# Second feed-forward of a two-layer gated cross-attention block: tokens sorted by expert, one expert per tile, in place of all experts masked

## The reference, cut to what matters

```python
def _L1_ffn_ref(x, gate_w, gate_b, W1, b1, W2, b2):
    logits = jnp.einsum('bld,de->ble', x, gate_w) + gate_b
    probs = jax.nn.softmax(logits, axis=1)
    idx = jnp.argmax(probs, axis=-1)
    out = jnp.zeros_like(x)
    for e in range(N_EXP):
        h = jax.nn.gelu(jnp.einsum('bld,df->blf', x, W1[e]) + b1[e], approximate=False)
        y = jnp.einsum('blf,fd->bld', h, W2[e]) + b2[e]
        out = out + jnp.where((idx == e)[..., None], y, jnp.float32(0.0))
    return out
...
x = x + jnp.tanh(g_xattn[1]) * _L1_xattn_ref(ctx_1024, _layernorm(x, axis=-1), ...)
x = x + jnp.tanh(g_ffn[1]) * _L1_ffn_ref(_layernorm(x, axis=-1), ...)
```

## Time and profile before

| | |
|---|---|
| median of 3 runs | 760.32 us (759.6 to 761.9) |
| profiled execution, device time | 757.69 us |
| its span | 755.6 us (2.1 us of the time lie around it) |
| busy share of the span | PE 93%, PEld 70%, DVE 73%, ACT 47%, POOL 45% |
| mean granted clock of TensorE | 0.986 of full speed |

### The profile page before, as it was taken

How to read it: one execution, slowest core, us unless ns; L and a number is a source line. 1 busy time by engine, 2 the same in 40 slices (tenths; PEclk the granted TensorE clock), 3 DMA queues, 4 the chain that set the end, 5 groups by cost and what they waited for, 6 DMA issues and landing times.

```text
span 755.6 us, 14538 instructions
## 1 busy us (share of the span) xinstructions
PE 699.8 (93%) x5642; PEld 530.3 (70%) x5642; DVE 552.8 (73%) x1089; ACT 356.9 (47%) x531; POOL 337.9 (45%) x421
## 2 busy tenths in 40 slices
PE   5789999999988898999999999999999988999896
PEld 5666666666877776767777677776777655887895
DVE  5767887774798877977668766688866886687544
ACT  3657667665344335555444445445534545120300
POOL 3374434410442215666656666567665774100000
PEclk9689999999999999999999999999999999999999
DMA  8100000000600030000000000000000000000000
GB/s 182 20 1 2 3 1 2 2 2 2 223 1 0 1 95 18 1 2 1 2 1 2 1 2 1 1 2 1 3 1 2 1 2 0 1 8 1 8 8 7
DMA packets 25586, 11.58 MB, mean 15 GB/s; under 512 B 11856, under 2 KB 24224, under 8 KB 25392
## 3 DMA queue, kind: packets, MB, share of 16 engines
q1 hardware_dynamic: 24512, 10.60, 5.5%
q10 hardware_dynamic: 1008, 0.07, 0.1%
HBM read 10.08 MB, written 0.52 MB: 14 GB/s over the span
## 4 chain that ended last, share of the span: by engine, by line
PE 72%; DVE 21%; issue 4%; ACT 1%; DMA 1%; SPq 0%; DVEq 0%; ACTq 0%
PE ps L1754 69%; DVE o L1458 3%; DVE pmax L1445 2%; DVE mx L1128 2%; PE ps L1765 1%; DVE kql L1433 1%; DVE exm L1324 1%; DVE ysum L1591 1%; DVE pmax L1442 1%; DMA raw<-in_L_xattn_Wproj_dram 1%; DVE rs_t L1005 1%; PE ps L1858 1%; DVE w_l L1666 0%; DVE sel L1584 0%; DVE wsel L1321 0%
## 5 line engine op out<-in xcount | busy, mean ns | idle before, releaser
L868 ACT ACTIVATE p<-ps 128x1024 f32<-128x1024 f32 x96 | 96.2, 1026 | 148.1 <-PE ps L1754 148.1
L1754 PE MATMUL ps<-p,v 128*64 128x256 f32 (+1 forms) x1280 | 125.0, 387 | 0.6 <-DVE xr L1154 0.6
L600 POOL TENSOR_TENSOR acc<-p 128x256 f32<-128x256 f32 x128 | 91.7, 748 | 74.8 <-ACT p L868 74.5
L1754 PE MATMUL ps<-kqh 64*128 64x256 f32 (+1 forms) x640 | 109.9, 369 | 13.2 <-DVE pmax L1442 3.5
L606 POOL TENSOR_TENSOR acc<-acc,p 128x256 f32<-128x256 f32 x128 | 92.0, 751 | 59.3 <-ACT p L868 59.2
L1442 DVE TENSOR_REDUCE pmax<-ps 128x2 f32<-128x1024 f32 x64 | 78.2, 1222 | 36.3 <-PE ps L1754 36.0
L1128 DVE TENSOR_REDUCE mx<-ps 128x1 bf16<-128x512 f32 x128 | 82.5, 687 | 25.1 <-PE ps L1754 24.4
L1754 PEld LDWEIGHTS ps<-p,v 128*64 128x64 f32 (+1 forms) x1280 | 66.8, 127 | 47.2 <-issue 16.5
L1754 PEld LDWEIGHTS ps<-kqh 64*128 64x128 f32 x640 | 61.7, 190 | 42.4 <-issue 34.6
L555 POOL TENSOR_SCALAR q<-qst,rmask 128x256 fp32r<-128x256 f32 x64 | 58.9, 940 | 58.3 <-ACT qst L628 58.3
L732 ACT ACTIVATE p<-ps 128x1024 f32<-128x1024 f32 x64 | 65.5, 1026 | 23.1 <-PE ps L1754 21.3
(11 more groups left out here) (294 smaller groups left out, 1587.5 us busy)
## 6 DMA issues: line engine op xcount, KB each, us to landing
w<-in_L_ffn_W_dram SPq DMA_DIRECT2D x1, 2048.0 KB, 12.0
wt<-in_L_ffn_W_dram SPq DMA_DIRECT2D x4, 512.0 KB, 6.1
ctx_all<-in_ctx_dram SPq DMA_DIRECT2D x4, 256.0 KB, 5.6
raw_kv<-in_L_xattn_Wkv_dram SPq DMA_DIRECT2D x1, 1024.0 KB, 4.8
raw<-in_L_ffn_B_dram SPq DMA_DIRECT2D x9, 64.0 KB
xr<-in_x_dram SPq DMA_DIRECT2D x4, 128.0 KB, 3.9
raw_q<-in_L_xattn_Wq_dram SPq DMA_DIRECT2D x1, 512.0 KB, 5.7
wout<-in_L_xattn_Wout_dram SPq DMA_DIRECT2D x1, 512.0 KB, 7.0
```

Source lines behind the costliest of these rows:

```text
L600: ins = pool.tensor_tensor(acc1[:, at], p1[:, s, 0, at], p1[:, s, 1, at], ALU.add)
L868: act.activation(p1[:, g % 2, u, :], bank(2 * (n % 2), 2), ACT.Exp, scale=SCALE1).then_inc(a_exp1.sem, 1)
L1754: return pe.matmul(o, lhsT, rhs, start=start, stop=stop)
```

## The change

Tokens are handled in two sets: batches 0 to 2 (768 tokens, 6 tiles) and batch 3 (256 tokens, 2 tiles). For each set, DVE and PE find the expert of every token, its rank among the tokens of that expert (a triangular matmul, `rank1`), and a slot: each expert's slots begin at a multiple of 128, so that a tile of 128 slots belongs to one expert. 768 tokens need at most 13 such tiles and 256 tokens at most 9, and all 22 are always computed. POOL scatters the normed tokens (`xnA`, `xnB3`) by slot number to scratch memory, one indirect transfer per 128 tokens (`scattered`); SP reads the slots back in groups of up to four tiles (`slots_in`); PE turns them (`slots_turn`), ACT and DVE split them (`slots_high`, `slots_low`). PE reads the number of each tile's expert into registers (`experts_in`) and takes that expert's weights through an address in a register. For a tile `up1` has 4 matmuls of 512 columns, `hidden_turn` 4 transposes, `down1` 4 of 256 columns and 5 of 128. The result `y1` of each tile is written to scratch memory (`slots_out`), and when a set is done POOL gathers the rows of its tokens (`gathered`, 6 and 2 indirect transfers), DVE adds them to `xr` and SP writes them out.

Besides: the low and high parts of W1 are now made in attention steps 8 to 10 and 14 to 18, one expert in each, and those of W2 in steps 29 to 31; batch 2's `outputs1` goes one step ahead; routing of the first set goes into steps 24 to 31. The scatter of the first set stands on POOL ahead of the sums of step 31.

```diff
+    SETS = (range(B - 1), range(B - 1, B))
+    TOKEN_TILES = tuple(TQ * len(z) for z in SETS)
+    SLOT_TILES = tuple((n * P + E * (P - 1)) // P for n in TOKEN_TILES)
...
+        W1_PAIRS = (8, 9, 10, 14, 15, 16, 17, 18)
+        W2_PAIRS = (G1 - 3, G1 - 2)
+        TURN_SLOTS = (1, 5, 9, 11, 14, 18)
...
+            def scattered(z, of):
+                pool.wait_ge(s_zero.sem, 32)
+                pool.wait_ge(d_route.sem, d_route.after(z, 4))
+                for t in range(TOKEN_TILES[z]):
+                    pool.indirect_dma_start(
+                        out=xs_dram[z], out_offset=bass.IndirectOffsetOnAxis(ap=slot_u[z][:, t:t + 1], axis=0),
+                        in_=of[:, t, :], in_offset=None).then_inc(s_scatter[z].sem, 16)
...
             for g in range(G1):
                 s = g % 2
+                if g == G1 - 1:
+                    scattered(0, xnA)
...
+            spread_hot(0)
+            scattered(1, xnB3)
+            spread_hot(1)
+            gathered(0)
+            gathered(1)
...
+            slots_high(0)
+            gelu(0)
+            for tile in range(SLOTS_ALL):
+                if tile + 1 < SLOTS_ALL:
+                    gelu(tile + 1)
+                hidden_high(tile)
+                if tile >= 1:
+                    output_part(tile - 1)
...
+                if tile == 5:
+                    softmax(1)
+            output_part(SLOTS_ALL - 1)
...
+                mm(o, xs_h[:, tile, :], of_expert(w1_h), True, False)
+                mm(o, xs_h[:, tile, :], of_expert(w1_l), False, False)
+                mm(o, xs_l[:, tile, :], of_expert(w1_h), False, False)
+                mm(o, hot[:, tile, :], biases_hl[:, 0:F], False, True).then_inc(e_up.sem, 1)
...
+            expert = list(experts_in(0))
+            slots_turn(0)
+            up1(0)
+            outputs1(B - 1)
+            for tile in range(SLOTS_ALL):
+                if tile + 1 < SLOTS_ALL:
+                    up1(tile + 1)
+                hidden_turn(tile)
+                if tile >= 1:
+                    down1(tile - 1)
+                if tile in TURN_SLOTS:
+                    slots_turn(TURN_SLOTS.index(tile) + 1)
...
+                if tile == SLOT_TILES[0] - 2:
+                    expert += list(experts_in(1))
+            down1(SLOTS_ALL - 1)
```

More of the change, by code:

```diff
@@ L219, in flamingo @@
[L219 to L226, removed]
@@ L494, in _ @@
+            sp.wait_ge(s_scatter[1].sem, 16 * TOKEN_TILES[1])
+            for k in range(len(first_groups), len(GROUPS)):
+                slots_in(k)
+            for tile in range(6, SLOTS_ALL - 3):
+                slots_out(tile)
             for b in range(B - 1):
@@ L496, in _ @@
                 sp.dma_start(out_v[b], x_of(b)).then_inc(s_out.sem, 16)
+            for tile in range(SLOTS_ALL - 3, SLOTS_ALL):
+                slots_out(tile)
             for t in range(TQ):
@@ L908, in _, with softmax, second_high @@
+            def softmax(z):
+                rows = ROWS * len(SETS[z])
+                act.wait_ge(d_route.sem, d_route.after(z, 1))
+                act.activation(probT[0:rows, :], probT[0:rows, :], ACT.Exp, bias=sm[0:rows, 1:2],
+                               accum_out=sm[0:rows, 2:3]).then_inc(a_route.sem, 1)
+            def second_high(g, n):
+                if g in W2_PAIRS:
+                    w2_high(4 * W2_PAIRS.index(g) + n)
             for g in range(G1):
@@ new lines, in gelu, with hidden_high @@
+            def gelu(tile):
+                act.wait_ge(e_up.sem, tile + 1)
+                if tile == 0:
+                    act.wait_ge(g_acc.sem, g_acc.after(G1, 0))
+                if tile >= 2:
+                    act.wait_ge(e_hidT.sem, tile - 1)
+                act.activation(hid1[:, tile % 2, :], bank(UP_BANK[tile % 2]), ACT.Gelu).then_inc(a_gelu.sem, 1)
+            def hidden_high(tile):
+                act.wait_ge(e_hidT.sem, tile + 1)
+                if tile >= 2:
+                    act.wait_ge(e_down.sem, tile - 1)
+                    act.wait_ge(d_hidL.sem, tile - 1)
+                copy(hidT_h[:, tile % 2, :], bank(HID_BANK[tile % 2])).then_inc(a_hidH.sem, 1)
@@ L1218, in tokens_stats, with tokens_scale @@
                 own()
[L1220 to L1223 removed]
+            def tokens_scale(tiles, part, twice, lo=0):
+                vh, y, tmp = (a[:, lo:lo + tiles] for a in rs_tokens)
+                var = token_moments[:, lo:lo + tiles, 1]
                 if part == 0:
@@ L1751, in _ @@
+            output1(SLOTS_ALL - 1)
+            for t in range(TQ):
+                dve.wait_ge(s_y_tok[1].sem, 16 * TQ)
+                dve.scalar_tensor_tensor(out=x_of(B - 1)[:, t, :], in0=y_tok[:, TQ * (B - 1) + t, :], scalar=G_F1,
+                                         in1=x_of(B - 1)[:, t, :], op0=ALU.mult, op1=ALU.add).then_inc(d_xD.sem, 1)
         @block.tensor
```

883 lines of the change are left out of this document (474 added, 409 removed).

## The result

The changed kernel takes **725.65 us** (median of 4 runs, 724.0 to 726.61) against 761.11 us for the kernel before (4 runs beside it, 759.6 to 762.41): a ratio of 0.955, 95% interval 0.952 to 0.958. The forecast was 725 us. Its profiled execution took 726.61 us, with a span of 724.8.

The account below looks back on a forecast made before the run. PE's matmuls were taken to bound the feed-forward. The loop beginning at 648.9, 22 tiles of 2.6 us and the tail gave 720.3; 2.1 around the span and 2.6 for the median made 725 us, 8 in 10 within 707 to 749.

Parts of the forecast that it names:

- The median: Added to the total: the median of runs stood 2.6 us above the profiled execution of the kernel before.
- The transfers: Before the feed-forward loop, POOL's six scatters take 1.28 us each, 7.7 in all; bounds 0.34 and 2.4 each.
- The slot numbers: Ready when POOL ends step 30's fold, without a wait; DVE's eight small operations take 0.14 to 0.2 us each.
- The registers: PE reading 13 experts into registers before the loop costs 1.5 us, and nine for the second set 1.5.
- The tile: In the loop, 2.6 us each: 2.26 of PE's stream and 0.35 of handovers; bounds 2.26 and 3.45.
- What stands beside the tiles: In the loop, the second set's softmax table loads add 1.5 us to the path and nine registers 1.5.
- The step that failed: In the loop, the second set's routing, scatters and reading lie beside tiles 3 to 11, some 23 us.
- W1 on DVE is hidden: In attention steps, DVE's eight W1 low parts fit its 2.6 us of idle time a step; uncovered, 7 us.
- The late sequencer: Rival, chance 0.20: in the loop, six address instructions cost 0.84 us a tile, 18.5 in all; about 743 us.
- The covered case: Rival, chance 0.10: tiles at 2.26 us, scatters and gathers at 0.34, registers free; total 707 us.
- POOL at 2.4 us a transfer: Rival, chance 0.05: six scatters and two last gathers cost 9 us more, uncovered W1 rows 7; total 741 us.
- The clock in the loop: Rival, chance 0.05: PE's pauses bring the loop to 1.2 GHz, a tile to 4.85 us; 50 us more, 775.

Follow-up runs that it names:

- Run 8: Changed kernel with POOL sending the first set's six scatter transfers twice, the second time to scratch that nothing reads: 733.4 us, 7.75 more.
- run 1: Changed kernel with every tile's expert a program constant, so no register loads and no address work on the sequencer: 724.77 us.
- run 7: As run 6, with the transposes of the second set's first four slot tiles at the end of tile 10 instead of 11: 720.42 us.
- run 6: Changed kernel with the second set's expert picked from logits without softmax, the rest of its routing one tile earlier: 723.0 us, 2.65 less.
- run 3: Changed kernel with the second set's routing written one tile earlier in each engine's order: 725.93 us.
- run 9: Changed kernel with DVE's eight W1 low parts cut to 8 columns in the attention, tiles using W1's high part twice: 725.75 us.
- run 2: Changed kernel with step 31's sums moved from POOL to PE as 12 products with ones: 723.33 us, 2.3 less.
- run 5: Changed kernel with one of the four 512-column products left out of each tile: 723.65 us.
- run 11: run 10 plus run 3, second set's first slot transposes one tile earlier, its token normalisation earlier on DVE, softmax kept: 715.57 us, ratio 0.942 to the kernel before.
- run 12: run 11 plus slot numbers ahead of DVE's second W2 row and ten unused PE products while waiting for slots: 712.7 us, ratio 0.938 to the kernel before.
- run 4: Changed kernel with PE running 36 unused products of 512 columns while it waits for step 31's fold: 725.14 us.
- run 10: run 2 with the last projection written between the first slots' transposes and `up1(0)`: 718.53 us, 4.8 below run 2.

## Why the prediction was right, step by step

The total was right, and so was the mechanism: PE's stream set the feed-forward, and cutting it was worth 35 us. Several terms were off, and they nearly cancelled, so that 725 came within 0.7 us is luck. Positions of after are given less 3.7 us, by which the mark lies later than in the trace that the sum was made against.

| step | predicted | measured |
|---|---|---|
| fold of step 30 ends | 623.5 | 623.7 |
| wait for the slot numbers | 0 | 1.39 |
| six transfers on POOL | 7.7 | 7.9 |
| step 31's sums and fold | 7.3 | 7.0 |
| sums on PE, 13 registers | 2.1 | 1.5 |
| transposes, high and low part | 1.9 | 2.9 |
| `up1(0)` and projection, with the clock | 6.4 | 6.15 |
| loop begins | 648.9 | 650.6 |
| 22 tiles, softmax, 9 registers | 60.2 | 60.1 |
| from there to the end of the span | 11.2 | 10.4 |
| end of the span | 720.3 | 721.1 |

- **The median.** The 2.6 us that I added for the median over the profiled execution of before fits the difference at the start: that execution began early and after's late. 722.4 and 3.7 make 726.1, and the profiled execution of after took 726.61. I knew nothing of the two starts, so this term was right by luck.
- **The transfers** (1.28 from the nearest row of POOL, the bounds 0.34 and 2.4) measured 0.96 to 1.31 and 0.30 between them, 1.27 each. Run 8 shows that they pass to the end one for one. The gathers: 2.2 (predicted 2.6).
- **The slot numbers** were not ready by the fold's end, though I said that they would be. DVE's eight operations took 2.6 us, where 0.14 to 0.2 each make at most 1.6: one took 0.51, and the product that ends with the fold 0.67. So 0.5 us of the 1.39 pass before DVE is done, and 0.9 between DVE's end and POOL's start.
- **The registers** (1.5 each time): the loads take 1.29 and 0.86 us, but I put them on the path whole. They cost it 0.42 us for the 13 (run 1), the rest lying beside the fold's product, and nothing for the nine, which in run 7 lie beside a tile's matmuls. The Trainium skill (Runtime: NRT & Kernel Launch, Instruction fetch mechanics) gives some 200 ns for a register; here, where `expert_i` lies in SBUF, it is about 100 ns, so the measurement decides against it in this case.
- **The tile**, 2.6 of which 0.35 for handovers: 2.43 and no handover at all. The stream itself is 2.42, not 2.26 (a row of 512 columns 0.235 us behind the one before, `down1` 1.06 instead of 0.9). Over 22 tiles 3.7 us too much.
- **What stands beside the tiles** was too little by nearly the same, 3.6 us. I had 3.0 (softmax 1.5, registers 1.5). The loop's 60.1 us are 6.6 more than 22 times 2.43: 2.4 at tiles 6 and 7 (run 6: 2.1 by the softmax), 2.4 at `up1(13)`, and 3.3 for the slots' transposes (0.4 for four), the routing's own rows on PE and two short waits for DVE, which I hadn't counted at all; 1.5 come off, because the first turn of the loop has no `down1` and the last no `up1`.
- **The step that failed** is "its routing, its scatters and its reading lie beside tiles 3 to 11". The landing just did (688.0), but I didn't ask what stands between the transposes and their use: the code puts them directly ahead of `up1(13)`. Runs 3 and 7 show that this order, and not the landing, made the 1.50 us.
- **W1 on DVE is hidden**, as far as run 9 went (4.2 of 8.7 us); a low part took 1.09 us, where I had 0.9. Its cover, 2.6 us of idle time a step, was read rightly from the earlier trace rows.
- **The rivals.** The late sequencer falls with the 2.43 us, and with run 1. The covered case falls with POOL's 1.27 us and the tile's 2.42. POOL at 2.4 us a transfer is excluded by its rows. The clock in the loop: 1.00 from 659 us on, but runs 1, 2, 5, 11 and 12 have a tile at 0.50 behind pauses, so the mechanism exists for single tiles, at 1.6 us each.

What stays open: why the same pause of 1.50 us before `up1(13)` was followed by the lower clock in runs 1, 2 and 5 and not in after or in runs 3, 4, 6, 8, 9 and 10; why in runs 11 and 12 two pauses of 0.65 and 0.47 us ahead of tile 7 were followed by it, where after has 0.80 and 0.65 at tile 6 and stays at 1.00; and what passes in the 0.9 us between DVE's slot numbers and POOL's first transfer, for which no run was made.

## What to carry to other kernels

- Where a kernel hands work from one phase to the next through memory, look at what the code puts directly ahead of the first use: a transposition one step too late cost 1.5 us that no earlier landing could win back, and one changed number removed it.
- Work that comes to stand behind new transfers on the issuing engine is delayed by all of them (7.9 us here); if another engine idles for that long, give it that work, here 12 matmuls in place of 7.0 us.
- A pause on PE can cost twice, as a wait and as a lower clock after it: fill it with work that has to be done anyway (the projection) before filling it with work for nothing.

## What the runs showed of the chip

- **An address from a register is free beside matmuls:** 2.43 us a tile with and without. Loading the registers takes about 0.10 us each (1.29 us for 13, 0.86 for nine); beside the fold's product 0.42 us of it showed, beside a tile's matmuls nothing (run 7).
- **An indirect transfer of 128 rows holds POOL for 0.96 to 1.31 us, and the next begins 0.30 us later,** and in the loop it is 0.95 to 1.01. In every run the first of the six takes 1.22 us and the third 1.31; whether DVE's work beside them does that, as I weighed, no run shows.
- **DVE waits for POOL where both operands lie in SBUF.** The Trainium skill (SBUF — State Buffer, SBUF: two separate sides) says that such an operation and one of POOL that reads SBUF take a shared pair of ports in turn, each for the whole instruction. The rows agree. Beside one fold of the changed kernel (it ends at 617.30) DVE has two operations of the same size, the first with an operand in PSUM (`ps`), the second with both in SBUF:

```profile
616.03 1.27 POOL L757 TENSOR_TENSOR fold<-acc 128x512 f32<-128x512 f32 x1
...
616.65 0.21 DVE L1693 TENSOR_TENSOR same<-ps,top 128x48 f32<-128x48 f32 x1
616.89 0.48 DVE L1695 TENSOR_TENSOR same<-same,order 128x48 f32<-128x48 f32 x1
```

The first takes 0.21 us, the second ends 0.07 us after the fold. The product of `same` and `one_hot` ended 0.06 to 0.07 us after its fold whether DVE had begun the slot operations 2.1 or 2.7 us before the fold's end. The other way round, POOL's sums lost 0.46 us beside DVE's row of W2 (runs 11 and 12). All this is read from rows, and no run took POOL's fold away.
- **The clock can fall after a pause of 1.5 us, and need not;** in runs 11 and 12 it fell after two of 0.65 and 0.47 us. In the loop it cost 1.6 us when it did, in the projection up to 1.9 (5.67 in run 3 against 3.74 in run 12).
- **Two executions can differ by some 3 us before the second attention begins,** more than most edits here were worth.
